# Stacking the first block's q parts on their own, and projecting the second superblock into three idle banks

## The reference

```
q, k, v = x@Wq+bq, x@Wk+bk, x@Wv+bv          # 16 heads for q, 4 groups for k and v
scores  = q.k / sqrt(16)                      # masked: key later than query, or 128 or more before it
y  = layernorm(x + softmax(scores)@v @ Wo + bo)
xr = mu_r*y + (1-mu_r)*y_prev ;  xk = mu_k*y + (1-mu_k)*y_prev
out = layernorm(y + sigmoid(xr@W_r) * (square(relu(xk@W_k)) @ W_v))
```

## Time and profile before

| | |
|---|---|
| median of 3 runs | 511.7 us (510.95 to 513.18) |
| profiled execution | 514.49 us, its span 512.8 us |
| busy, share of the span | PE 81%, DVE 66%, POOL 57%, ACT 53%, PEld 49% |
| mean granted TensorE clock | 0.902 |
| DMA | 39.24 MB, mean 77 GB/s |

### The profile page before, as it was taken

The page is one execution under the profiler, slowest core; times in us unless marked ns, Lnnn a source line. Parts: engine busy times, 40 slices in busy tenths (PEclk is TensorE's granted clock), DMA queues, the critical chain, the costliest instruction groups (busy, mean ns, idle before and its releaser), DMA issues.

```text
span 512.8 us, 8346 instructions
## 1 busy us (share of the span) xinstructions
PE 413.8 (81%) x2494; PEld 253.1 (49%) x2494; DVE 340.2 (66%) x851; ACT 272.8 (53%) x566; POOL 290.0 (57%) x466
## 2 busy tenths in 40 slices
PE   5407767998699959998699958998699949999963
PEld 2105344565356545565356545565355635666452
DVE  5315534588577848788497848688578838888543
ACT  3301334665447735775367735775467725787642
POOL 5500334565557736675477736675567737777721
PEclk9856567999889978999799999999899969999988
DMA  7770493035802384034902384045902390000000
GB/s 287 140 90 7 112 150 59 7 82 92 155 11 66 75 136 91 12 83 94 168 13 64 76 131 98 11 87 94 164 13 66 74 133 13 13 12 24 22 10 31
DMA packets 49356, 39.24 MB, mean 77 GB/s; under 512 B 32160, under 2 KB 40864, under 8 KB 49184
## 3 DMA queue, kind: packets, MB, share of 16 engines
q1 hardware_dynamic: 42256, 25.73, 21.7%
q10 hardware_dynamic: 7056, 12.98, 16.7%
HBM read 26.38 MB, written 12.06 MB: 75 GB/s over the span
## 4 chain that ended last, share of the span: by engine, by line
PE 45%; DVE 19%; DMA 19%; ACT 5%; issue 5%; SPq 4%; POOL 1%; ACTq 1%; DVEq 0%; POOLq 0%
DMA qs<-max_rows 11%; PE av_ps L963 8%; PE proj_ps L876 8%; PE score_ps L949 7%; DMA qs<-q_parts 6%; PE gen L1054 5%; DVE neg_max L688 5%; PE max_ps L932 4%; PE gen L1043 4%; SPq L321 3%; PE gen L997 3%; DVE mix L763 3%; DVE q_tiles L680 2%; DVE y L782 2%; PE gen L1032 2%
## 5 line engine op out<-in xcount | busy, mean ns | idle before, releaser
L386 POOL TENSOR_SCALAR_AFFINE_SELECT probs<-probs 128x512 f32<-128x512 f32 x252 | 167.5, 674 | 156.4 <-ACT probs L521 154.0
L521 ACT ACTIVATE probs<-score_ps 128x512 f32<-128x512 f32 x252 | 148.5, 598 | 139.8 <-PE score_ps L949 118.3
L949 PE MATMUL score_ps<-qs,ks 98*128 98x512 bf16 x252 | 102.4, 408 | 45.3 <-DMA qs<-max_rows 27.5
L688 DVE TENSOR_REDUCE neg_max<-max_ps 128x3 f32<-128x480 f32 x144 | 87.5, 632 | 24.7 <-PE max_ps L932 24.2
L949 PEld LDWEIGHTS score_ps<-qs,ks 98*128 98x128 bf16 x252 | 25.0, 100 | 108.2 <-ACT probs L521 57.5
L963 PE MATMUL av_ps<-probs,vals 128*32 128x512 f32 x504 | 70.5, 634 | 0.9 <-POOL probs L386 0.8
L932 PE MATMUL max_ps<-ks,q_tiles 96*128 96x160 bf16 x416 | 55.6, 254 | 0.0
L876 PE MATMUL proj_ps<-x_t,first 128*128 128x512 f32 x88 | 47.2, 663 | 9.3 <-DMA first<-w_first 5.5
L763 DVE SCALAR_TENSOR_TENSOR mix<-diff,first,x_t 128x128 f32<-128x128 f32 x128 | 50.7, 440 | 0.0
L393 POOL TENSOR_TENSOR rstd<-var,minus_half 128x1 f32<-128x1 f32 x64 | 35.7, 558 | 18.7 <-DVE var L712 17.7
L378 POOL TENSOR_TENSOR parts<-rest,parts 128x512 bf16<-128x512 f32 x24 | 30.3, 1266 | 27.7 <-ACT parts L503 27.7
(11 more groups left out here) (74 smaller groups left out, 631.4 us busy)
## 6 DMA issues: line engine op xcount, KB each, us to landing
qs<-q_parts ACTq DMA_DIRECT2D x48, 256.0 KB, 9.7
q_parts<-parts SPq DMA_DIRECT2D x48, 128.0 KB, 2.2
x_t<-x_feat SPq DMA_DIRECT2D x8, 512.0 KB, 11.9
x_in<-x_nat SPq DMA_DIRECT2D x8, 512.0 KB, 15.3
out<-out_t SPq DMA_DIRECT2D x32, 128.0 KB, 1.7
ks<-k_parts SPq DMA_DIRECT2D x42, 80.0 KB, 2.9
qs<-max_rows SPq DMA_DIRECT2D x128, 2.0 KB
k_parts<-parts SPq DMA_DIRECT2D x8, 192.0 KB, 2.8
```

The lines of the kernel that those rows point to most:

```text
L386: nc.gpsimd.affine_select(out=v, in_=v, compare_op=ALU.is_ge if i % 2 else ALU.is_gt, fill=0.0, base=0, pattern=[[0, HPG], [sign, BLK]], c ...
L521: nc.scalar.activation(probs[:, buf, i], score_ps[i % 2][:, :], ACT.Exp, scale=SCALE).then_inc(s_exp, 1)
L688: nc.vector.tensor_reduce(neg_max[:, TPB * i:TPB * i + n], max_bank(t, j, i)[:, 0:n * TILE_KEYS].rearrange("p (n k) -> p n k", k=TILE_KEYS ...
L949: nc.tensor.matmul(score_ps[i % 2][:, :].rearrange("p (h q) -> p h q", q=BLK), ks[0:ROWS + MPARTS, par, g, k0:k0 + BLK], qs[0:ROWS + MPART ...
```

## The change

On the q parts of superblock 0: ACT no longer issues six DMAs of four blocks each. It issues six of block 0 alone (64 KB), counted with the six ks DMAs by a new semaphore `s_stack0`. SP waits for all twelve and issues six for blocks one to three (192 KB), counted by `s_stack`. The tile copy of block 0 waits for `s_stack0`; that of block 1 for `s_stack`, and it is moved behind `turn_max(0, 0)` on DVE.

On superblock 1: its three chunks go into gen0, gen1 and av_ps, which nothing uses yet, back to back on PE ahead of block 0's maxima, and v is turned there too. The waits that protected `proj_ps` go, and `v_turn(1)` waits for the value copy of superblock 0. ACT takes the high parts as they come, the third ahead of the stacking DMAs, and two of the middle parts behind them. DVE takes all three rests and the value copy ahead of `tile_q(0)`. POOL's `x_plus_bo` is moved behind low parts. Later superblocks are unchanged, apart from the count awaited on `s_stack`.

```diff
@@ sync, stack_k
-                    sp.dma_start(ks[rep * DH:(rep + 1) * DH, par, :, WINDOW:], src[:, :, 0:SB]).then_inc(s_stack, 16)
+                    sp.dma_start(ks[rep * DH:(rep + 1) * DH, par, :, WINDOW:], src[:, :, 0:SB]).then_inc(s_stack0, 16)
@@ sync, start
                 for rep in range(NREP):
                     stack_k(0, 0, rep)
+
+                sp.wait_ge(s_stack0, STACKS)
+                for rep in range(NREP):
+                    sp.dma_start(qs[rep * DH:(rep + 1) * DH, 0, 1:].rearrange("d j (m x) g t -> d (j m) (x g t)", m=QCH),
+                                 q_dram[0, Q_PART[rep], 1:].rearrange("j m (d y) t -> d (j m) (y t)", d=DH)
+                                 ).then_inc(s_stack, 16)
                 max_in(0, 0, 0)
@@ gpsimd, start
-                x_plus_bo(0, 0)
                 for m in range(NCH):
                     low_part(0, m)
+                x_plus_bo(0, 0)
+                low_part(1, 0)
                 x_plus_bo(1, 1)
-                for m in range(NCH):
-                    low_part(1, m)
+                low_part(1, 1)
+                low_part(1, 2)
@@ scalar, start
                 middle_part(0, NCH - 1)
-                high_part(1, 0)
+                high_part(1, 0, gen0)
+                high_part(1, 1, gen1)
+                middle_part(1, 0)
+                high_part(1, 2, av_ps)
+                act.wait_ge(s_spill_q, SPILLS)
                 for rep in range(NREP):
-                    stack_q(0, 0, rep)
-                middle_part(1, 0)
-                high_part(1, 1)
+                    act.dma_start(qs[rep * DH:(rep + 1) * DH, 0, 0].rearrange("d (m x) g t -> d m (x g t)", m=QCH),
+                                  q_dram[0, Q_PART[rep], 0].rearrange("m (d y) t -> d m (y t)", d=DH)
+                                  ).then_inc(s_stack0, 16)
                 middle_part(1, 1)
-                high_part(1, 2)
                 middle_part(1, 2)
@@ vector, tile_q
-                if j == 0:
-                    dve.wait_ge(s_stack, s * STACKS + STACKS)
+                if s == 0 and j == 0:
+                    dve.wait_ge(s_stack0, STACKS)
+                elif j == (1 if s == 0 else 0):
+                    dve.wait_ge(s_stack, s * STACKS + STACKS // 2)
@@ vector, start
-                rest_part(1, 0)
-                rest_part(1, 1)
+                rest_part(1, 0, gen0)
+                rest_part(1, 1, gen1)
+                rest_part(1, 2, av_ps)
+                val_copy(1, 1)
                 tile_q(0, 0, 0, 0)
-                tile_q(1, 0, 1, 0)
                 for i in range(NMAXB):
                     tile_max(0, 0, i)
                 turn_max(0, 0)
-                rest_part(1, 2)
-                val_copy(1, 1)
+                tile_q(1, 0, 1, 0)
@@ tensor, project_chunk
-                    if later(s, 1):
+                    if later(s, 2):
                         pe.wait_ge(s_val, s)
@@ tensor, v_turn
-                pe.wait_ge(s_rest, s * NCH + (NCH if later(s, 1) else 1))
+                if s == 1:
+                    pe.wait_ge(s_val, 1)
+                else:
+                    pe.wait_ge(s_rest, s * NCH + (NCH if later(s, 1) else 1))
@@ tensor, start
-                for m in range(QCH):
-                    project_chunk(1, m, 1)
+                for m in range(NCH):
+                    project_chunk(1, m, 1, (gen0, gen1, av_ps)[m])
+                v_turn(1)
                 pe.wait_ge(s_zero, 5)
                 pe.wait_ge(s_masks, 2 + TPB)
                 for i in range(NMAXB):
                     max_scores(0, 0, 0, i)
-                    if i == 1:
-                        project_chunk(1, QCH, 1)
-                v_turn(1)
                 pe.wait_ge(s_restw, 16)
```

More of the change, by code:

```diff
@@ L177, in attention_channel_mix @@
         s_stack = sem("s_stack")
+        s_stack0 = sem("s_stack0")
         s_tiles = sem("s_tiles")
```

## The result

The changed kernel takes 498.42 us by the median of four runs (497.25 to 500.94), against 511.44 us of the kernel before (510.95 to 513.18). The ratio is 0.9746, with a 95% interval of 0.9702 to 0.979: 2.5% faster, 13.0 us. The forecast was 501.5 us, 10.2 us faster, in a range of 498 to 507.5. The sign, the place and the mechanism were right. The size was short by 2.8 us, and the time lies at the low end of the range.

The account below looks back on a forecast made before the run. The prediction took the first two superblocks' q-part landings as the bound. Gains of 9.1, 0.40 and 1.25 us, together 10.7, less 0.5 for luck, gave 10.2 off 511.7: 501.5 us, range 498 to 507.5.

Parts of the forecast that it names:

- What bounds, and where: Start functions: landings of the first two superblocks' q parts, at 37.1 and 83.65 us, hold everything up; no later superblock's do.
- First set: Block 0's q parts on ACT: issued from 21.2 us, 0.9 us lost to three ACT operations, complete at 26.7 (26.0 to 31.4).
- Second set: Blocks one to three on SP: first DMA 3.9 us, five more at 1.54 each, landing at 38.35 us (37.8 to 40.6).
- Under the transfer: Block 0's maxima start at 27.55 us and rows are ready at about 33, while the rest of q lands.
- the 5 us of cover: Block 0's rows ready at about 33 us, 5 us before the rest of q lands.
- SP's queue: Behind SP's new wait: no issuing stall, k spill landed at about 40 us, k stacks hidden with 1 to 2 us spare.
- the sum: Block 1's maxima 9.1 us earlier, plus waits of 0.40 and 1.25: together 10.7, less 0.5 for luck, 10.2 us.
- Passing on: From max_in(1) onward order and gaps stay as before, so the 83.65 us landing comes 10.2 us earlier, later stretches moving too.
- rival 1: Second q transfer on SP slower or starting later: landing 2.3 to 6 us later, time 504 to 508, about 506; chance 0.15.
- rival 4: Slower kernel: SP's queue carries the transfer at under half the rate; break-even about 62 GB/s, 516.5 us at 50; chance 0.03.
- rival 2: Second q transfer runs at the input loads' 427 GB/s, landing at 31.6 us: gain 14 to 16, time 496; chance 0.03.
- rival 3: Head start not passed on: the transfer ending at 83.65 us ends unchanged, time stays 511.7, within 2.6; chance 0.05.

Follow-up runs that it names:

- the split alone: Kernel before with only the q stacking split, block 0 first and blocks one to three on SP, superblock 1 projected as before: 503.17 us, ratio 0.9777.
- the doubled second set: Changed kernel with six more 192 KB DMAs issued by SP ahead of those for blocks one to three: 508.32 us, ratio 0.9921 to the kernel before.
- the second trace of the changed kernel: Changed kernel run once more, unaltered, beside other experiments: 499.1 us, ratio 0.9744 to the kernel before.

## Why the prediction was right, and short

**What bounds, and where.** Right: both landings of q parts held the kernel before, and the first now ends 12 us earlier for what waits on it. From ACT's first issue of superblock 1 to its copy it is 19.6 us, where 19.4 were carried over, so that the copy came at 69.77 instead of near 73.

**First set.** Forecast complete at 26.7, measured 25.40. The spills landed 0.4 us earlier, by chance. Of the other 0.9, 0.7 is the charge of 0.9 us for three ACT operations ahead of the issues: they cost 0.2 us, because ACT's issues went out among them. The row at 64.25 against 64.59 had shown that an issue can go ahead of one operation; it went ahead of two. The last 0.2 is the landing of the last 64 KB, 2.98 us against 3.2.

**Second set, the mis-sized term.** Forecast 11.6 us from the first issue to the last landing, bounds 11.0 and 13.9; measured 9.95, below the lower bound. The first and the last of the six (KB, us to landing):

```profile
qs<-q_parts SPq DMA_DIRECT2D x1, 192.0 KB, 3.5
...
qs<-q_parts SPq DMA_DIRECT2D x1, 192.0 KB, 7.7
```

The first took 3.5, the low bound, and the others followed 1.28 us apart, 154 GB/s, where I scaled the 2.0 us of a 256 KB DMA down to 1.54. In the six other traces with this set as it is it took 10.1, 10.3, 10.5, 10.7, 10.7 and 11.4 us. The time differs between executions by a seventh, and bounds from one trace, in which ks DMAs shared the engines, were too narrow.

**Under the transfer.** Block 0's maxima began at 26.50, and its rows were ready at 32.52, 6.0 us later against 5.2 to 5.6; the 5 us of cover were 2.9, still enough. The projection's move cost nothing and, by the split alone, brings 1.25 us at the first score.

**SP's queue.** Right in each step: no stall in issuing, the k spill landed at 38.3 and max_in(1) was issued at its rows. The slack of 1 to 2 us was 0.2, so here it was close. From block 1's maxima to the first score 8.8 us passed, where the sum has 9.0 (39.2 to 48.2).

**Passing on.** Right, by the doubled second set: 9.2 us later at the end, by the medians, for 7.9 to 9.2 at the start.

**What was missing.** The granted clock behind the wait at 83.65: 2.5 us in this pair of traces, less in others. I saw the wait and not the slow clock that stands behind it. I took 0.5 us off for luck where a term with the other sign was due. The four pieces, 0.9 + 0.4 in the first set, 1.65 in the second and 2.5 of clock, come to 5.5 us, more than the 2.8 us by which the forecast was short. The same trace lost 2.8 us again behind its peak, by scatter, and the second trace of the changed kernel has less of them (landing 0.75 us slower, clock half lost). So part of how near the forecast came is luck.

**The rivals.** A slower set on SP (rival 1) and one at under half the rate (rival 4) were not seen in any trace. The rate of the input loads (rival 2) wasn't either: 154 GB/s at best. The Trainium skill (DMA: Bandwidth & Descriptors, Anatomy of one DMA) gives its fit for DMAs that GpSimd issues; these, issued by SP, took twice the 5 us or so that the prediction worked out from it. The head start was passed on, against rival 3. Rival 4's break-even is mis-worked: by the sum's own form (26.7 + 3.9 + five DMAs) a landing at 49.1 is 3.7 us for each DMA of 192 KB, 53 GB/s and not 62; the rival had 0.03, and nothing hung on it.

## What to carry to other kernels

When a transfer holds up the first use of a small part of it, send that part first and let the rest run under the work on it; a change in the prologue is then worth its microseconds one for one, if a chain of waits leads from there to the end. Look past the wait at the clock behind it: here part of the extra in the trace was work at 1.2 GHz behind a wait that went away. And look at what small DMAs on another queue wait for: cutting large transfers in two gave more than twice what this change gave.

## What the runs showed of the hardware

- Small DMAs on one queue land late when another queue is full of large ones: four of 2 KB took 7.6 to 9.7 us to land behind DMAs of 256 KB in the two traces of the changed kernel, and mostly 4 to 5.5 us behind DMAs of 128 KB, against 1.75 alone. Whether it is the size of the large ones or the bytes issued ahead that counts, these runs don't tell. The Trainium skill (DMA: Bandwidth & Descriptors, Queues, rings and completion order) tells of engines that go round their queues a packet at a time; no view here shows single packets, so these runs don't test it.
- DMAs that write 16 partitions from DRAM, 2 KB in a run, moved 123 to 154 GB/s while one followed another (192 KB in 1.60 to 1.28 us), from ACT's queue as from SP's, with the engines' share at about 1; the input loads moved 392 to 440 GB/s in stretches of 2 us at the same share.
- An issue holds ACT about as long as it is: 0.45 to 0.73 us. Eleven in a row held its computing for 6.1 us.
